# Last layer of a four-layer program: the order of its combined per-slot program, its PSUM banks and its buffers are changed

## The reference, cut to what matters

```python
# x: (16, 112, 512); Wa: (512, 1536 after its parts are put together); Wp: (512, 512)
fused = layernorm(x) @ (Wa * col_scale)         # q, k (16 heads of 32), v
scores = q @ k.T / sqrt(32)                     # per sequence and head: 112 x 112
scores = where(causal, scores, lowest)
attn = softmax(scores)
y = (attn @ v) @ Wp
out = x + tanh(g_ffn[1]) * y
```

## Time and profile before

| | |
|---|---|
| median of 3 runs | 2336.24 us (2332.31, 2336.24, 2336.58) |
| the profiled execution | 2331.43 us, span 2329.7 us |
| mean granted TensorE clock | 0.959 of full speed over the span |
| TensorE matmuls busy | 2148.5 us, 92% of the span |
| VectorE, ScalarE, GpSimd busy | 1274.8, 1167.8, 664.3 us |
| DMA | 205.96 MB, mean 88 GB/s |

### The profile page before, as it was taken

The page is one execution under the profiler, slowest core; times in us unless marked ns, Lnnn a source line. Parts: engine busy times, 40 slices in busy tenths (PEclk is TensorE's granted clock), DMA queues, the critical chain, the costliest instruction groups (busy, mean ns, idle before and its releaser), DMA issues. The chain is left out here.

```text
span 2329.7 us, 38459 instructions
## 1 busy us (share of the span) xinstructions
PE 2148.5 (92%) x13464; PEld 1742.0 (75%) x13464; DVE 1274.8 (55%) x2475; ACT 1167.8 (50%) x3025; POOL 664.3 (29%) x814
## 2 busy tenths in 40 slices
PE   6999999999989999999889959999999977888887
PEld 4777777777768888888668848888888866666665
DVE  4555555555534543653355547777777754444444
ACT  4666666665643333443234337766767733333333
POOL 1423424334311000000034435555555530111111
PEclk9999999999999999999989979999999998889897
DMA  4434436344255210100043432332222312101000
GB/s 142 146 86 146 133 87 201 102 144 118 84 161 213 77 55 1 64 28 1 30 137 108 128 122 97 101 100 92 96 80 82 100 45 75 32 20 37 17 25 25
DMA packets 167397, 205.96 MB, mean 88 GB/s; under 512 B 63680, under 2 KB 105664, under 8 KB 166752
## 3 DMA queue, kind: packets, MB, share of 16 engines
q1 hardware_dynamic: 167264, 204.15, 27.9%
HBM read 128.13 MB, written 75.99 MB: 88 GB/s over the span
## 5 line engine op out<-in xcount | busy, mean ns | idle before, releaser
L1696 POOL TENSOR_TENSOR c_probs<-c_probs,c_rsum 112x375 f32<-112x375 f32 x256 | 212.8, 834 | 232.3 <-DVE c_rsum L1806 226.5
L1802 DVE TENSOR_REDUCE c_nmax<-c_score 112x1 f32<-112x375 f32 x256 | 136.1, 533 | 98.8 <-PE c_score L1872 98.8
L536 ACT ACTIVATE a_probs<-a_score,a_nmax 112x375 f32<-112x375 f32 x256 | 144.0, 571 | 59.6 <-DVE a_nmax L690 59.6
L1750 ACT ACTIVATE c_pT_hi<-c_turned 125x336 fp32r<-125x336 f32 x256 | 115.4, 451 | 109.4 <-PE c_turned L1880 109.3
L1191 ACT ACTIVATE b_silu<-b_gate,b_ug_scale 128x512 f32<-128x512 f32 (+1 forms) x64 | 40.7, 635 | 250.7 <-PE b_up L1297 250.6
L543 ACT ACTIVATE a_pT<-a_turned 125x672 f32<-125x672 f32 x128 | 93.6, 731 | 134.1 <-PE a_turned L878 134.1
L2057 POOL TENSOR_TENSOR f_probs<-f_probs,f_rsum 112x448 f32<-112x448 f32 x64 | 59.7, 933 | 345.2 <-DVE f_rsum L2173 345.2
L1248 DVE SCALAR_TENSOR_TENSOR b_hidden<-b_up,b_ug_scale,b_silu 128x512 f32<-128x512 f32 (+1 forms) x64 | 43.7, 683 | 204.3 <-ACT b_silu L1191 204.3
L1743 ACT ACTIVATE c_probs<-c_score,c_nmax 112x375 f32<-112x375 f32 x256 | 148.0, 578 | 0.0
L847 PE MATMUL a_shared<-a_w_lo,a_kT_hi 128*125 128x512 f32 x384 | 134.2, 431 | 0.0
L1880 PEld LDWEIGHTS c_turned<-keep_ident,c_probs 112*125 112x125 f32 x768 | 122.4, 189 | 15.7 <-POOL c_probs L1696 6.7
(11 more groups left out here) (311 smaller groups left out, 5973.8 us busy)
## 6 DMA issues: line engine op xcount, KB each, us to landing
q<-q_qT SPq DMA_DIRECT2D x14, 1024.0 KB
c_q_raw<-q SPq DMA_DIRECT2D x16, 896.0 KB
k<-ab_stage SPq DMA_DIRECT2D x16, 752.0 KB, 4.1
c_k_raw<-k SPq DMA_DIRECT2D x16, 752.0 KB
v<-ab_stage SPq DMA_DIRECT2D x48, 250.0 KB
c_v_raw<-v SPq DMA_DIRECT2D x16, 750.0 KB
ab_lead<-in_ctx_dram SPq DMA_DIRECT2D x16, 672.0 KB
wug<-a_ug_turned SPq DMA_DIRECT2D x32, 256.0 KB, 3.8
```

What stands on the lines that cost most here:

```text
L536: last = act.activation(probs[:, n % 2, i, :], score[0:S, i, 0:T], ACT.Exp, bias=nmax[:, b % 2, h:h + 1], accum_out=sums[:, b % 2, h:h + 1])
L1696: pool.tensor_tensor(probs[:, h % AHEAD, :], probs[:, h % AHEAD, :], rsum[:, p, h:h + 1].broadcast_to([S, T]), ALU.mult).then_inc(scaled, 1)
L1750: act.activation(pT[0][:, g % 2, :, j, :], src, ACT.Copy).then_inc(pT_hi, 1)
L1802: dve.tensor_reduce(nmax[:, p, h:h + 1], score[h % AHEAD][0:S, 0:T], axis=AX.X, op=ALU.max, negate=True).then_inc(max_done, 1)
```

## The change

In every engine's list the steps are moved:

- TensorE: `weigh(t - 2)` in the place of `weigh(t - 1)`; the projection of sequence b is in slot 4b + 6 (`finished`) instead of 4b + 5, behind the block of its slot; the loop has 4 slots after the last instead of 2.
- VectorE's slot t: `finish(b - 1)` at i = 3, `probs_copy(t - 1)`, `reciprocal(t + 1)`, `maximum(t + 2)`, the low part of the output at i = 1, the low parts of the blocks of slot t-1. Four normalisations in a row, in slots 5 and 21 (for the group after next).
- ScalarE's slot t: the high part of the output at i = 1, the high parts of the blocks of slot t-1, `exps(t + 2)`.
- Banks: from the fourteenth use on, blocks and projections take work[0] and work[1] in turn (`uses` is the list of all of them in the order of the program); `free_bank` waits for the use two before.
- xT has two buffers (one for each of two groups), v is a ring of 6 sequences.
- Tables: q3 and k3 are made ahead of slot 0. The x blocks of a group come in slots -10, -6, -2 and 2 (counted from 16 (g - 1)), for group 1 in slots 1, 2, 2 and 3. The other 12 blocks come one a slot in slots 4, 5, 7, 8, 9, 11, 12, 13, 15, 16, 17 and 19: three in four slots, and the fourth slot has the projection and an x block.
- SP loads the normalised inputs of a third group at the start, and the next group's after the fourth sequence of a group has been stored.

```diff
-    SETS, RING = 2, 3
+    SETS, RING, V_RING = 2, 3, 6
-    START = {-1: "x0 x1 x2 x3 q0 k0 q1 k1 v0 q2 k2", 0: "q3 k3", 1: "v1", 2: "v2", 3: "v3"}
+    START = {-1: "x0 x1 x2 x3 q0 k0 q1 k1 v0 q2 k2 q3 k3", 0: "v1", 1: "v2", 3: "v3"}
-    LATER = {4: "x0 x1", 5: "x2 x3", 6: "q0", 7: "k0", 8: "q1", 9: "k1", 10: "v0", 11: "q2", 12: "k2", 13: "q3", 14: "k3",
-             15: "v1", 16: "v2", 18: "v3"}
+    SECOND_TURNED = {1: "x0", 2: "x1 x2", 3: "x3"}
+    TURNED = {-10: "x0", -6: "x1", -2: "x2", 2: "x3"}
+    LATER = {4: "q0", 5: "k0", 7: "q1", 8: "k1", 9: "v0", 11: "q2", 12: "k2", 13: "q3", 15: "k3", 16: "v1", 17: "v2", 19: "v3"}
...
+    def finished(t):
+        return [b for b in range(B) if t == G * b + G + 2]
...
+    uses = [use for t in range(-1, SLOTS + G) for use in items(t) + [(b, "y") for b in finished(t)]]
...
-            n = number(g, name) - 1
-            return (work, tail, turned, outp)[n % 4] if n < FIRST else work
+            n = uses.index((g, name))
+            return (*work, turned, outp)[n % 4] if n < FIRST else work[n % 2]
...
@@ scalar
-            for t in range(SLOTS + 2):
+            for t in range(SLOTS + G):
                 b, i = divmod(t, G)
                 if i == 1 and b:
                     out_hi(b - 1)
-                if t + 1 < SLOTS:
-                    exps(t + 1)
-                for g, name in items(t):
+                for g, name in items(t - 1) if t else []:
                     item_hi(g, name)
+                if t + 2 < SLOTS:
+                    exps(t + 2)
...
@@ vector
-            for t in range(SLOTS + 3):
+            for t in range(SLOTS + G):
                 b, i = divmod(t, G)
+                if i == G - 1 and b:
+                    finish(b - 1)
+                if 0 < t <= SLOTS:
+                    probs_copy(t - 1)
+                if t + 1 < SLOTS:
+                    reciprocal(t + 1)
+                if t + 2 < SLOTS:
+                    maximum(t + 2)
                 if i == 1 and b:
                     out_lo(b - 1)
-                if i == 2 and b:
-                    finish(b - 1)
-                if t + 2 < SLOTS:
-                    maximum(t + 2)
-                if t + 1 < SLOTS:
-                    reciprocal(t + 1)
-                for g, name in items(t):
+                for g, name in items(t - 1) if t else []:
                     item_lo(g, name)
...
-                if t < SLOTS:
-                    probs_copy(t)
-                if t % 16 < BPG and t // 16 + 1 < NG:
-                    normalize(BPG * (t // 16 + 1) + t % 16)
+                if t % 16 == 5 and t // 16 + 2 < NG:
+                    for n in range(BPG):
+                        normalize(BPG * (t // 16 + 2) + n)
@@ tensor
-                n = number(g, name) - 1
-                used = n - 4 if n < FIRST else n - 1
-                if used >= 0:
-                    pe.wait_ge(work_hi, used + 1)
-                    pe.wait_ge(work_lo, split_number(*order[used]))
+                n = uses.index((g, name))
+                used = n - 4 if n < FIRST else n - 2
...
+                if uses[used][1] == "y":
+                    pe.wait_ge(x_done, uses[used][0] + 1)
+                else:
+                    pe.wait_ge(work_hi, number(*uses[used]))
+                    pe.wait_ge(work_lo, split_number(*uses[used]))
...
-            for t in range(SLOTS + 2):
-                b, i = divmod(t, G)
+            for t in range(SLOTS + G):
                 if t + 2 < SLOTS:
                     scores(t + 2, 0)
-                if 0 < t <= SLOTS:
-                    weigh(t - 1)
+                if 2 <= t < SLOTS + 2:
+                    weigh(t - 2)
                 if t + 2 < SLOTS:
                     scores(t + 2, 1)
                 for g, name in items(t):
                     run_item(g, name)
-                if i == 1 and b:
-                    project(b - 1)
+                for b in finished(t):
+                    project(b)
                 if t < SLOTS:
                     turn(t)
```

More of the change, by code:

```diff
@@ L1945, in items @@
         for g in range(1, NG):
-            found += [(g, name) for name in LATER.get(t - 16 * (g - 1), "").split()]
-        return found
+            turned_too = SECOND_TURNED if g == 1 else TURNED
+            for table in (turned_too, LATER):
+                found += [(g, name) for name in table.get(t - 16 * (g - 1), "").split()]
+        return found
+    def finished(t):
+        return [b for b in range(B) if t == G * b + G + 2]
     order = [item for t in range(-1, SLOTS) for item in items(t)]
+    uses = [use for t in range(-1, SLOTS + G) for use in items(t) + [(b, "y") for b in finished(t)]]
     FIRST = len(items(-1))
@@ L1978, in phase_d @@
         score = m.ps("score", [P, 2 * SETS, 512])
-        work, tail, turned, outp = (m.ps(n, [P, 512]) for n in ("work", "tail", "turned", "outp"))
+        work = [m.ps(f"work{n}", [P, 512]) for n in range(2)]
+        turned, outp = (m.ps(n, [P, 512]) for n in ("turned", "outp"))
         w_loaded = {name: m.sem(f"w_loaded_{name}") for name in weights}
@@ L2039, in _ @@
                 load_residual(b)
-            for b in range(BPG, 2 * BPG):
+            for b in range(BPG, 3 * BPG):
                 load_normal(b)
@@ L2113, in _ @@
             weights_hi("k2")
+            weights_hi("q3")
             item_hi(0, "q2")
-            weights_hi("q3")
-            item_hi(0, "k2")
             weights_hi("k3")
-            for t in range(SLOTS + 2):
+            exps(1)
+            for name in ("k2", "q3", "k3"):
+                item_hi(0, name)
+            for t in range(SLOTS + G):
                 b, i = divmod(t, G)
@@ L2189, in finish @@
                     dve.wait_ge(x_stored[p], 16 * (b // 2))
-                dve.scalar_tensor_tensor(out=xout[:, p, :], in0=tail[0:S, :], scalar=keep["gates"][0:S, 3:4], in1=xin[:, p, :],
+                dve.scalar_tensor_tensor(out=xout[:, p, :], in0=bank(b, "y")[0:S, :], scalar=keep["gates"][0:S, 3:4], in1=xin[:, p, :],
                                          op0=ALU.mult, op1=ALU.add).then_inc(x_done, 1)
@@ L2238, in free_bank @@
             def free_bank(g, name):
-                n = number(g, name) - 1
-                used = n - 4 if n < FIRST else n - 1
-                if used >= 0:
-                    pe.wait_ge(work_hi, used + 1)
-                    pe.wait_ge(work_lo, split_number(*order[used]))
+                n = uses.index((g, name))
+                used = n - 4 if n < FIRST else n - 2
+                if n in (FIRST, FIRST + 1):
+                    used = max(u for u in range(FIRST) if bank(*uses[u]) is work[n % 2])
+                if used < 0:
+                    return
+                if uses[used][1] == "y":
[3 more added lines that the diff above has]
+                    pe.wait_ge(work_lo, split_number(*uses[used]))
             def run_item(g, name):
@@ L2261, in run_item @@
                         if name[0] == "v":
-                            last = pe.matmul(out[0:S, :], xT[s][:, c, n * S:(n + 1) * S], w[r][:, c, 2 * D:], **flags)
+                            last = pe.matmul(out[0:S, :], xT[s][:, g % 2, c, n * S:(n + 1) * S], w[r][:, c, 2 * D:], **flags)
                         else:
-                            last = pe.matmul(out[:, 0:GS], w[s][:, c, weight_of(name)], xT[r][:, c, :], **flags)
+                            last = pe.matmul(out[:, 0:GS], w[s][:, c, weight_of(name)], xT[r][:, g % 2, c, :], **flags)
                 last.then_inc(work_ready, 1)
@@ L2301, in weigh @@
                 if t == 0:
[L2302 removed]
+                    pe.wait_ge(work_lo, split_number(0, "q3"))
                 if i == 0:
@@ L2308, in weigh @@
                     h = HPG * i + n
-                    last = pe.matmul(outp[rows(n), i * S:(i + 1) * S], v[:, g % 2, j, h * HD:(h + 1) * HD], pT[:, t % 2, n, :],
+                    last = pe.matmul(outp[rows(n), i * S:(i + 1) * S], v[:, b % V_RING, h * HD:(h + 1) * HD], pT[:, t % 2, n, :],
                                      start=True, stop=True)
@@ L2322, in project @@
                     for c in range(DC):
-                        last = pe.matmul(tail[0:S, :], oT[s][:, c, :], wp[r][:, c, :], start=n == 0 and c == 0,
+                        last = pe.matmul(bank(b, "y")[0:S, :], oT[s][:, c, :], wp[r][:, c, :], start=n == 0 and c == 0,
                                          stop=n == len(PASSES) - 1 and c == DC - 1)
```

31 lines of the change are left out of this document (17 added, 14 removed).

## The result

| | before | changed |
|---|---|---|
| median | 2334.27 us (4 runs, 2327.42 to 2336.58) | 2294.43 us (4 runs, 2289.08 to 2296.12) |
| span of the profiled execution | 2329.7 us | 2291.7 us |
| last layer in it (from VectorE's memset of the scores) | 415.5 us | 371.6 us |

The ratio is 0.983, 95% interval 0.9803 to 0.9858: 1.7% faster, 39.8 us by the medians. The untouched layers began the last one at 1914.2 us before and at 1920.1 us after; that difference of 6 us also occurs between two executions of one kernel (1920.1 and 1914.4 for the changed one).

A forecast was written before the change was run, and what follows sets the result against it. TensorE was taken to bound the last layer except its tail, with waits and a lowered clock. Start +1.0, slots 4-19 +1.1, 20-35 +0.5, 36-51 -25.5, tail -2.2: -25.1 us; forecast 2310 us, inner range 2300 to 2320, outer 2286 to 2332.

The forecast's parts named there:

- Sums two slots late: TensorE's waits ahead of the sums for turned probabilities (pT, 32.9 us) and for the attention output's split (oT, 19.3) go.
- The two new waits: Slots 4 to 35: 2.12 us ahead of the block after an x block, 1.52 ahead of some projections; 11.5 per stretch.
- q0 of slot 4 waits for x3's split: After the start, the q0 block in slot 4 is held up 2.1 us by the split of block x3.
- Slot prices: TensorE's work per slot without waits: q/k block 4.27 us, projection 4.60, v block 4.61; an x block adds 0.60.
- normalisations: Four in a row on VectorE in slots 5 and 21, some 2.5 us, half hidden: +1.3 us each time.
- The clock in the x stretches: Slots 4 to 19 and 20 to 35, which have x blocks: clock falls in quiet stretches cost 10 us each.
- The last stretch: Slots 36 to 51, no x blocks: nothing idles, clock holds, 2 us allowed for falls; 73.0 us against 98.48, -25.5.
- Rival 1: The clock keeps falling in slots 36 to 51; 16 to 18 us of the gain don't come: 2326 us, chance 0.14.
- Tail and start: Tail, the last twelve slots: -2.2 us; start, slots 0 to 3: +1.0 us.
- The loop of 2.87 us: Mask and maximum, exponentials, reciprocal and hand-overs form a loop of 2.87 us that paces the tail's empty slots.
- rival 2: The clock holds everywhere; new waits cost only themselves, 10 us less per x stretch, 5 in tail: 2286 us, chance 0.18.

The follow-up runs named there:

- the second profile: The changed kernel, no edit, profiled a second time: last layer 379.7 us, ratio to before 0.9795-0.9851.
- own_slot: The changed kernel with each block's high and low parts made in the block's own slot again: last layer 337.5 us, ratio to before 0.9628-0.9693.
- split_first: The changed kernel with the blocks' low parts ahead of maximum(t + 2) in VectorE's slot: last layer 340.9 us, ratio to before 0.9663-0.9695.
- x_first: The changed kernel with only the x blocks' low parts ahead of the maximum: last layer 352.8 us, ratio to before 0.9682-0.9746.
- pipe_only: The kernel before with sums two slots late, copy first, projection and finish one slot later; old splits, banks, tables: layer 364.2 us, ratio 0.9742-0.9801.

## Why the prediction was right, and where it was too small

Direction and mechanisms held for the parts that the sum has; the gain in the profiled layer was 43.9 us against 25.1 in the sum (35.8 in the second profile), and by the medians 39.8 against 26.

- *Sums two slots late.* Right: the waits for pT and oT are gone from slots 4 to 51. With this and the copy's new place alone the layer gains 51 us, and the whole change without it gains none. It is not all that helps: own_slot gains 78 us, 27 more than the pipeline alone.
- *The two new waits.* Right in place, number and cause: eight ahead of the block after an x block, 1.96 instead of 2.12 us; four ahead of projections, 1.87, 1.47, 1.76 and 1.48 against 1.52. That q0 of slot 4 waits for x3's split held too (2.0).
- *Slot prices: mis-sized.* I took the idle time off the slots of the earlier trace rows (the one of the earlier trace rows is slot 24, not 23, when a slot runs from turning to turning). In slots 36 to 51 a q/k slot lasts

```profile
2182.91 0.55 PE L2319 MATMUL f_turned<-keep_ident,f_probs 112*112 112x112 f32 x4
...
2187.15 0.55 PE L2319 MATMUL f_turned<-keep_ident,f_probs 112*112 112x112 f32 x4
```

4.24 us (4.21 in others) and not 4.27, a v block's or a projection's 4.53 and not 4.61; an x block adds 0.34, not 0.60 (slot 10 lasts 4.87): 0.60 is the length of its row, and the next matmuls start 0.37 us after it does. With waits and normalisations (1.3 counted, about 0.2 seen), the two x stretches without falls come to 85.4 and 83.3 us against 88.3 and 86.2.
- *The clock in the x stretches.* The step was 10 us each; measured 3.1 and 8.8, then 10.2 and 8.8: 7.7 in the mean. The size was near for three of four; that slots 4 to 19 fell so seldom in the first profile is luck, 7 us of it. split_first and x_first show that the waits cause the falls.
- *The last stretch.* 70.1 against 73.0: the allowance of 2 us was not needed; the clock was 1.00. Rival 1 is refuted here: its stretch cycles through two banks for sixteen slots and never lost the clock, and TensorE idles nowhere in it (busy 70.14 of 70.14 us). "TensorE: Matmul & The Clock Gate" of the Trainium skill, section "A second HAM failure mode: psum-queue depth-cycling", tells of a kernel that cycles through PSUM banks, idles briefly between groups of matmuls and has a swinging clock. The last stretch shows that cycling without the idling keeps the clock; the x stretches, with waits of 1.5 to 2 us, agree with the page.
- *Tail and start.* -3.6 against -2.2; +0.4 against +1.0. The loop of 2.87 us is as worked out, but the tail's sum was near by errors that cancel: the ten mask intervals took 38.5 us and not 37.1, and the first of these masks comes 2.8 us ahead of the tail's beginning where before it came 0.1 behind, which the sum did not have.

Of the miss of 18.8 us, 5.8 are slot prices in the x stretches, 8.1 the clock there, 2.9 the last stretch, 2.0 tail and start. The median of 2294 lies nearer to rival 2 (2286), 8 us off the other way, than to the forecast of 2310, 16 us off: with no fall in slots 4 to 35 the layer would have been 11.9 us shorter.

Of the signs that the prediction named, the waits, the clock from slot 36 on and the 2.87 us between masks of the tail came; that stretch took 70.1 us, just under the 71 to 75, and slots 4 to 19 moved by 8.7 us in the first profile where 5 was the most expected (1.7 in the second).

What the prediction did not see: it added up the parts, and never asked which of them was needed. The late splits cost 34 to 42 us of what the rest gave.

## What to carry to other kernels

When a consumer is moved a slot later, move only what waits: a release (here the split that frees a bank) that is moved along with it, behind a step that depends on the same slot's work, puts its full chain ahead of the next user of the buffer. Put on an in-order engine first what frees a buffer and needs nothing of this slot. Price a wait on TensorE twice, itself and the clock it may lose: own_slot has 20 us less of waits in slots 4 to 35 (3.9 against 24.3) and is 31 us shorter there than the changed kernel in its first profile, 38 in its second.

## What the runs showed of the hardware

The same program, with waits equal to 0.02 us, lost the clock at seven places in one execution and at ten in another, 7 us of difference in one stretch of sixteen slots. Of the 26 waits of 1.5 to 2.0 us ahead of blocks and projections in these two profiles (slots 4 to 35) 17 lost it. The eight waits of 0.44 us in split_first never did; its slot 22, with waits of 0.76 and 0.55 us, did (8.02 us, clock 0.79), and slot 6, with 0.73 and 0.66, did not (6.56 us, clock 1.00). What comes ahead of a wait matters as well: before the change, nine q/k slots with 1.0 us of idle time kept the clock, and in pipe_only a wait of 1.05 us just behind a slot without any block lost it three times out of three (slots of 11.5 us, clock 0.70). In 70 us without a gap it was never lost (1.00 in both profiles), although more than a third of each slot there (1.67 of 4.24 or 4.53 us) is short score and sum products and transposes.
